# Seven half products for Q in the last block of a gated cross-attention kernel

## The reference, cut to what matters

```
Q = layernorm(x) @ Wq.T ;  K = ctx @ Wk.T ;  V = ctx @ Wv.T
P = softmax(causal(Q K^T / sqrt(128)))         4 query heads share one K and V
x = x + tanh(g_xattn) * (P V) @ Wd.T
x = x + tanh(g_ffn) * (layernorm(x) @ dequantize(qweight).T + bias)
```

## Time and profile before

| what | value |
|---|---|
| median of 3 runs | 1058.12 us |
| the profiled execution, time | 1056.85 us |
| its span, first to last instruction | 1054.9 us |
| mean granted TensorE clock | 0.995 |
| PE busy | 1017.7 us, 96% |
| DVE busy | 682.1 us, 65% |
| ACT busy | 456.6 us, 43% |
| POOL busy | 233.9 us, 22% |
| moved by DMA | 142.61 MB, mean 135 GB/s |

### The profile page before, as it was taken

The page is one execution under the profiler, slowest core; times in us unless marked ns, Lnnn a source line. Parts: engine busy times, 40 slices in busy tenths (PEclk is TensorE's granted clock), DMA queues, the critical chain, the costliest instruction groups (busy, mean ns, idle before and its releaser), DMA issues.

```text
span 1054.9 us, 19976 instructions
## 1 busy us (share of the span) xinstructions
PE 1017.7 (96%) x7842; PEld 569.2 (54%) x7842; DVE 682.1 (65%) x1374; ACT 456.6 (43%) x917; POOL 233.9 (22%) x245
## 2 busy tenths in 40 slices
PE   5889999999999999999999999999999999999995
PEld 3455555555555555555555554555555555555542
DVE  6856677777577666765466556755556664555678
ACT  5767676676533243333334333244433322333322
POOL 1355565465604000210002100210000300000013
PEclk9999999999999999999999999999999999999998
DMA  7757645445355632345422743333432443224111
GB/s 278 235 153 272 216 163 182 161 135 157 102 178 196 149 90 66 141 133 137 132 71 70 206 134 121 109 119 93 131 122 108 133 137 126 62 86 143 64 36 60
DMA packets 90219, 142.61 MB, mean 135 GB/s; under 512 B 31248, under 2 KB 64016, under 8 KB 79504
## 3 DMA queue, kind: packets, MB, share of 16 engines
q1 hardware_dynamic: 90128, 141.34, 42.0%
HBM read 94.11 MB, written 25.17 MB: 113 GB/s over the span
## 4 chain that ended last, share of the span: by engine, by line
PE 87%; DVE 7%; ACT 3%; issue 2%; DMA 1%; SPq 0%; DVEq 0%; ACTq 0%
PE pa L1295 42%; PE py L1295 30%; PE av L1408 5%; PE pp L1391 3%; PE ps L1375 2%; PE py L1466 2%; PE pp L1375 2%; DVE q L897 1%; DVE sc L943 1%; DMA raw_q<-in_wqT 1%; DVE sc L954 1%; DVE row_max L941 1%; DVE sc L937 1%; ACT q L677 1%; PE av L1442 0%
## 5 line engine op out<-in xcount | busy, mean ns | idle before, releaser
L1295 PE MATMUL pa<-xT,wq 128*128 128x512 f16 x1536 | 342.7, 379 | 9.5 <-DVE q L897 6.7
L1295 PE MATMUL py<-wd,att 128*128 128x512 f16 x1488 | 336.2, 379 | 0.8 <-issue 0.8
L1295 PEld LDWEIGHTS pa<-xT,wq 128*128 128x128 f16 x1536 | 145.8, 98 | 189.9 <-issue 22.5
L1295 PEld LDWEIGHTS py<-wd,att 128*128 128x128 f16 x1488 | 143.3, 98 | 159.1 <-issue 1.1
L677 ACT ACTIVATE q<-pa 128x512 f16<-128x512 f32 x128 | 75.7, 591 | 264.3 <-PE pa L1295 264.3
L976 DVE SCALAR_TENSOR_TENSOR xacc<-py,f_y,xacc 128x512 f32<-128x512 f32 x128 | 95.7, 747 | 125.0 <-PE py L1295 124.9
L728 ACT ACTIVATE att<-av 128x256 f16<-128x256 f32 x256 | 80.8, 384 | 145.7 <-PE av L1408 145.2
L967 DVE SCALAR_TENSOR_TENSOR att<-av,att 128x256 f16<-128x256 f32 x256 | 93.3, 416 | 67.1 <-ACT att L728 66.9
L897 DVE SCALAR_TENSOR_TENSOR q<-pa,q 128x512 f16<-128x512 f32 x128 | 87.7, 685 | 57.0 <-ACT q L677 54.2
L1295 PE MATMUL pa<-wv,cT 128*128 128x128 f16 x1536 | 96.2, 219 | 0.0
L1295 PEld LDWEIGHTS pa<-wv,cT 128*128 128x128 f16 x1536 | 89.9, 98 | 0.9
(11 more groups left out here) (131 smaller groups left out, 1060.1 us busy)
## 6 DMA issues: line engine op xcount, KB each, us to landing
wq<-kept_q SPq DMA_DIRECT2D x24, 1024.0 KB, 7.1
wd<-kept_d SPq DMA_DIRECT2D x23, 1024.0 KB, 4.8
v_dup<-v_nat SPq DMA_DIRECT2D x128, 128.0 KB, 2.4
raw_d<-in_wdT SPq DMA_DIRECT2D x8, 1024.0 KB, 10.1
kept_q<-wq SPq DMA_DIRECT2D x8, 1024.0 KB, 8.8
kept_d<-wd SPq DMA_DIRECT2D x8, 1024.0 KB, 5.4
raw_q<-in_wqT SPq DMA_DIRECT2D x7, 1024.0 KB, 5.6
wk<-kept_k SPq DMA_DIRECT2D x24, 256.0 KB, 7.3
```

The source lines that it names most:

```text
L1295: last = pe.matmul(out, stationary(a, i), moving(b, i), start=(i == 0 and (a, b) == PASSES[0]), stop=(i == count - 1 and (a, b) == PASSES[ ...
```

## The change: what it does

The names below are those of the diff. `FIRST_FAST` is 24, so `fast(m)` holds for the Q of block 3 (m = 24 to 31), which is made in steps n = 23 to 30.

- **Seven products.** For m of block 3 and each pair r of heads, the product (2 heads) x (512 features) x (512 tokens) is cut in halves along all three: head, features 0-255 or 256-511, tokens 0-255 or 256-511. Instead of eight half products it makes seven (Strassen's scheme in Winograd's form). A half product (`run`) is 2 feature chunks x 3 passes = 6 matmuls of 256 columns. Their operands are partly sums of quarters of Wq (`ws`) and of the normalised x (`tT`). Products 1, 6, 7, 4 accumulate one after another in one bank; ACT copies products 1, 5 and the sum 1+6 to SBUF in between, and the DVE adds the others to them. Each quarter then gets its high part on ACT and its low part on DVE.
- **Sums of weights.** In steps 7, 12, 13, 14, 15, 17, 18, 21 (one group each) SP loads the raw Wq of a group (`load_mix`, 1 MB), POOL makes four sums (`mix_weights`), ACT and DVE make high and low parts (`mix_hi`, `mix_lo`, four each), SP stores 1 MB (`keep_mix`). From step 22 `back_mix` loads 1 MB for each m of block 3. The squares of Wq are taken with scale 2, and `Q_SCALE` is twice what it was.
- **Sums of x.** In step 20 POOL adds quarters of the normalised block 3 (`mix_norm`, `mixed_lo`), ACT makes the high parts (`mixed_hi`); 32 more DMA transposes go out in steps 21 and 22, and 8 of the 32 of norm (1, 3) are left out.
- **Order.** Norm (1, b) of blocks 2 and 3 moves from step g = 4 to g = 3, the step of the feed-forward; its transposes go out from g = 4 on (six in g = 3 for block 3). Norm (2, 2) is made for tiles 0 and 1 in step 24 and for 2 and 3 in step 25. From step 22 on, the output parts 2 and 3 of step n are made in step n+1, between the half products (`deferred`), and `back_d(n)` goes out in the middle of step n. `ffn_zero` of block 2 moves from step 25 to step 26, ahead of `av_part`.
- **Memory.** `xs` and the mixed tiles lie in `raw_k` and `raw_v` joined; `ws`, `tT` and `raw_s` lie in `raw_q` and `raw_d`; the feed-forward's part goes to `xs` and no longer to `xn`.

```diff
+        def fast(m):
+            return FIRST_FAST <= m < STEPS
+        def deferred(n):
+            return fast(n + 2)
+        BANK_X, BANK_Y, BANK_Z = (pa[0], av[1]), (pa[1], pa[1]), (av[0], av[0])
+        MIX_STEPS = (7, 12, 13, 14, 15, 17, 18, 21)
...
+            def run(m, r, i):
...
+                elif (r, i) == (1, 5):
+                    pe.wait_ge(c12_ok, pair_count(m, 0))
+                elif (r, i) == (1, 2):
+                    pe.wait_ge(c11_ok, pair_count(m, 0))
+                elif i == 6:
+                    pe.wait_ge(p1_ok, pair_count(m, r))
+                elif i == 7:
+                    pe.wait_ge(u2_ok, pair_count(m, r))
+                elif i == 3:
+                    pe.wait_ge(p5_ok, pair_count(m, r))
+                elif i == 4:
+                    pe.wait_ge(c22_ok, pair_count(m, r))
...
+                for kc in range(2):
+                    for c, d in PASSES:
...
+                        last = pe.matmul(half(bank), a[:, c, head, w_half + kc, :], b[:, d, b_half + kc, at],
...
# TensorE, step n with fast(m)
                 score_unit(n, 0)
                 score_unit(n, 1)
+                if fast(m):
+                    run(m, 0, 1); run(m, 0, 5); run(m, 0, 2); run(m, 0, 6)
+                    y_unit(n - 1, 2)
+                    run(m, 0, 7); run(m, 0, 3); run(m, 1, 1); run(m, 0, 4)
+                    run(m, 1, 5); run(m, 1, 2); run(m, 1, 6)
+                    y_unit(n - 1, 3)
+                    run(m, 1, 7); run(m, 1, 3)
+                    p_transpose(n, 0)
+                    run(m, 1, 4)
+                    k_unit(m)
+                    p_transpose(n, 1)
+                    v_unit(m, range(TILES // 2))
+                    av_unit(n, 0); av_unit(n, 1)
+                    v_unit(m, range(TILES // 2, TILES))
+                    y_unit(n, 0); av_unit(n, 2); y_unit(n, 1); av_unit(n, 3)
...
# VectorE, the same step
+                    scores(n, 0); scores(n, 1)
+                    add_11(m, 0)
+                    normalise(n, 0)
+                    add_22(m, 0); add_12(m, 0)
+                    lo_11(m, 0); lo_22(m, 0); lo_12(m, 0)
+                    normalise(n, 1)
+                    lo_21(m, 0)
+                    p_part(n, 0)
+                    y_late(2)
+                    p_part(n, 1)
+                    add_11(m, 1)
+                    y_late(3)
+                    add_22(m, 1); add_12(m, 1)
+                    lo_11(m, 1); lo_22(m, 1); lo_12(m, 1); lo_21(m, 1)
+                    k_part(m)
+                    if g == 2 and tb == BLOCKS - 1:
+                        for t in LATE: ffn_zero(t)
...
# ScalarE, the same step
+                    copy_p1(m, 0); exp(n, 0); copy_p5(m, 0); copy_u2(m, 0); exp(n, 1)
+                    hi_11(m, 0); p_part(n, 0); hi_22(m, 0); hi_12(m, 0)
+                    copy_p1(m, 1); hi_21(m, 0); p_part(n, 1); copy_p5(m, 1); copy_u2(m, 1)
+                    hi_11(m, 1); hi_22(m, 1); hi_12(m, 1)
+                    p_transposed(n, 0)
+                    hi_21(m, 1)
+                    k_part(m)
```

More of the change, by code:

```diff
@@ L242, in norm_of, with split_norm @@
             return None
+        def split_norm(n):
+            return n % GROUPS == 0 and fast(n + 1) and n < LAST
         def wait_x_lo(eng, t):
@@ L271, in transposed @@
             else:
-                eng.wait_ge(xT_ld, 16 * 2 * KC * TILES * (call - 1))
-        def dma_tiles(n):
-            g, tb = n % GROUPS, n // GROUPS
[L278 to L282, removed]
+                eng.wait_ge(xT_ld, 16 * sum(len(transposes(c)) for c in range(2, call + 1)))
@@ new lines, in build, with quadrant, by_batch, mixing @@
+        BANK_X, BANK_Y, BANK_Z = (pa[0], av[1]), (pa[1], pa[1]), (av[0], av[0])
+        def quadrant(c, r, head, tokens):
+            return q[:, c, tokens * BPB // 2:(tokens + 1) * BPB // 2, :, 2 * r + head, :]
+        def by_batch(part):
+            return part.rearrange("p (b u s) -> p b u s", b=BPB // 2, u=HALVES)
+        MIX_STEPS = (7, 12, 13, 14, 15, 17, 18, 21)
+        MIX_ORDER = tuple((FIRST_FAST + i) % GROUPS for i in range(GROUPS))
+        def mixing(n):
+            return MIX_STEPS.index(n) if n in MIX_STEPS else None
@@ new lines, in mix_of, with transposes @@
+        def mix_of(n):
+            g, tb = n % GROUPS, n // GROUPS
+            return tb + 1 if g == 4 and FIRST_BLOCK <= tb + 1 < BLOCKS else None
+        def transposes(call):
+            return [(t, c, i) for t in range(TILES) for c in (HI, LO) for i in range(KC)
+                    if NORMS[call][0] == 2 or not fast(GROUPS * NORMS[call][1]) or t < 2 or i >= 2]
+        EARLY, FEW = 6, 5
+        MIXED = ([(t, c, i) for t in (2, 3) for c in (HI, LO) for i in range(KC)]
+                 + [(t, c, i) for i_half in ((0, 1), (2, 3)) for t in (0, 1) for c in (HI, LO) for i in i_half])
@@ new lines, in transpose_early, with load_mix @@
+            def transpose_early(n):
+                g, tb = n % GROUPS, n // GROUPS
+                if g == 3 and 0 < tb < BLOCKS - 1 and fast(GROUPS * (tb + 1)):
+                    call = NORMS.index((1, tb + 1))
+                    transpose_norm(call, transposes(call)[:EARLY])
+            def load_mix(g):
+                if g == 0:
+                    sp.wait_ge(wd_lo, HPG * (GROUPS - 1))
+                    sp.wait_ge(wd_hi, HPG * (GROUPS - 1))
+                else:
+                    sp.wait_ge(s_lo, HPG * g)
+                sp.dma_start(raw_s, wqT[MIX_ORDER[g]].rearrange("p (h n) -> p h n", h=HPG)).then_inc(s_ld, 16)
@@ L443, in _ @@
                     back_d_last()
-                if GROUPS <= n < LAST:
+                if GROUPS <= n < LAST and not fast(m):
                     back_d(n)
@@ L570, in _ @@
                     ln_rstd(call)
+                if ffn_of(n) is not None and fast(n + 1):
+                    for t in range(ffn_of(n) * TILES, (ffn_of(n) + 1) * TILES):
+                        ffn_add(t)
                 if tb == 0:
@@ new lines, in quad_hi, with hi_11, hi_22, hi_12 @@
+            def quad_hi(ready, count, r, head, tokens, part):
+                act.wait_ge(ready, count)
+                return act.activation(quadrant(HI, r, head, tokens), by_batch(part), ACT.Copy, scale=Q_SCALE)
+            def hi_11(m, r):
+                quad_hi(c11_ok, pair_count(m, r), r, 0, 0, p1[:, r, :]).then_inc(quad_hi_ok, 1)
+            def hi_22(m, r):
+                quad_hi(c22_ok, pair_count(m, r), r, 1, 1, p5).then_inc(quad_hi_ok, 1)
+            def hi_12(m, r):
+                quad_hi(c12_ok, pair_count(m, r), r, 0, 1, u2).then_inc(quad_hi_ok, 1)
@@ L821, in _ @@
                     ctx_squares(tb + 1, squares_done(g + 2) + 2 if tb == 0 else squares_done(GROUPS))
+                if mix_of(n) is not None:
+                    for t in range(TILES):
+                        mixed_hi(mix_of(n), t)
                 if call is not None:
@@ L1110, in ffn_scaled @@
                 dve.wait_ge(f_mm, t + 1)
-                bank, part = (pa, xs) if t in LATE else (py, xn)
+                if t % TILES == 0 and t > 0 and t not in FFN_DVE:
+                    dve.wait_ge(out_pool, t)
+                    if t // TILES + 2 > FIRST_BLOCK:
+                        mixed_done(dve, t // TILES + 2 - FIRST_BLOCK)
+                bank, part = pa if t in LATE else py, xn if t in FFN_DVE else xs
                 dve.tensor_tensor(part[:, t % TILES, :], bank[t % 2][:, :], ff_rows[:, SCALE_ROW, :],
```

530 lines of the change are left out of this document (437 added, 93 removed).

## The result

| | median us | lowest to highest | runs |
|---|---|---|---|
| before | 1057.54 | 1056.66 to 1060.25 | 4 |
| after | 1047.59 | 1046.94 to 1048.74 | 4 |

The ratio is 0.9906 [0.9894, 0.9918]: 9.95 us less. Forecast were 1047.9 and 10.2. The profiled execution took 1048.74 us, its span 1046.9.

The account below looks back on a forecast made before the run. TensorE, busy 96%, was taken as the bound. Gain 11.5 less stalls 1.3, others 0, is 10.2 us off 1056.85: 1046.65, with 1.27 for the median 1047.9; range 1045.0 to 1051.5, to 1055 with the broken margin.

Parts of the forecast that it names:

- Term 1: Q in 8 fast steps of block 3: fewer columns, 10.58 to 9.14 us, 1.44 a step, 11.5 us gained.
- the rival with 0.140: Q's short matmuls paced by something other than columns, 0.140 us each: 1068.8 us, slower; chance 0.05.
- the loss of 15 us: Estimate from the skill's issue gaps, some 98 ns at 256 columns: Q 6.3 to 8.2 us, kernel 15 us slower.
- The walk: Plain fast step followed engine by engine: half additions at 0.4 us, no stall, tightest place (1,4) with 0.5 us.
- a thin margin that breaks: Rival, every fast step: DVE halves cost 0.12 more each, 0.45 us a step, 3.6 in all: 1051.5; chance 0.15.
- halves at the full price: Rival: DVE halves at 0.68 each, (1,4) waits 1.5 us in all 8 steps: 1059.9, no change; chance 0.05.
- Term 2: Steps 24 and 26, extra DVE work: stalls of 0.5 and 0.8 us, together 1.3, bounds 0 and 3.
- Term 3: Sums of weights in the weight steps: taken at 0, hidden, with wd loaded in time; 8 us were cover gone.
- Term 4: Changed order, chiefly steps 11 and 19 and the transposes on SP: taken at 0, bounds 0 to 1 in each step.
- the verdict that it changes nothing outside step 26: POOL and DVE excluding each other: DVE held 1.3 us once or twice a step, sum unchanged except in step 26.
- The place that I had watched: Step 19, P V part 3 ready at 674.3, fourth output part wants it at 674.55: 0.25 us to spare.
- Sum: Whole kernel: 11.5 - 1.3 = 10.2 us off, 1046.65 for the profiled execution, 1047.9 as median; forecast's chance 0.70.

Follow-up runs that it names:

- third experiment: Kernel before with only the order exchanged in plain steps from 8 on: low part of Q's head 1 ahead of both normalises, second exponential earlier; 1052.42 us, ratio 0.9943.
- first: Kernel after with product 5 of each pair made twice, so Q has as many columns as before; 1058.52 us, ratio 1.0007 against the kernel before.
- fourth experiment: Kernel after with two more 1 MB DRAM-to-DRAM copies ahead of each raw weight load; 1065.65 us, ratio 1.0068 against the kernel before.
- ninth: Kernel after without the six early transposes of step 19, all 24 issued in step 20; 1054.39 us, ratio 0.997 against the kernel before.

## Why the prediction was right, by its steps

**Term 1, right.** Predicted 1.44 per step, measured 1.40; the period 28.8 against 28.87. The columns are 0.109 us per 256 as read from P V (12 matmuls in 1.31), and no row shows anything else pacing short matmuls: the rival with 0.140 is out. So is the loss of 15 us that the prediction had estimated from the Trainium skill (TensorE: Matmul & The Clock Gate, "Back-to-back issue gap"). The wait that goes with `q_unit` is worth 0.2 (third experiment), the columns the rest (first).

**The walk, right, and thinly so.** The DVE's half additions take 0.41 to 0.43 (0.4 taken, of 0.36 to 0.68). In step 26 `add_22` of pair 1 is done at 866.80 and product (1,4) begins at 867.27: 0.47 us to spare where 0.5 was said. So "a thin margin that breaks" and "halves at the full price" are both out, the first by half a microsecond.

**Term 2, right in place and sum.** 0.32 in step 24 (0.5) and 0.97 in step 26 (0.8), 1.29 against 1.3.

**Term 3, right for time.** Steps 13 to 18 are unchanged to 0.01 us. The sums of the weights lie in ACT's and POOL's idle time. As for `wd`: it has landed in time everywhere, in 6.1 us (median) from its issue, 4.8 before, and the fourth experiment shows that two more MB would have made it late. But of the transposes of the sums of x, which share SP's queue with it, the prediction gave no margin, and it is 2.4 us. `back_d` of step 20 went out at t = 687.34 - 678.99 = 8.35 and not 7, and some of SP's loads took 1.05 us to issue, where most took 0.38. The conclusion held, over a margin that the prediction had not looked at.

**Term 4, wrong in size.** Taken at 0, measured 0.61 + 0.32 = 0.93 us. The place that I had watched, the fourth output part of step 19, holds: with the norm's four instructions between the two parts, steps 11 and 19 are unchanged. What I had not followed is POOL. The norm, moved into this step, puts four low parts ahead of POOL's residual adds, and they run on into the next step's scores. The rule of the Trainium skill (SBUF — State Buffer, "Who interferes with whom") about POOL and DVE was in the prediction, with the verdict that it changes nothing outside step 26; the overlap that costs something lies in the scores of steps 12 and 20, which the prediction didn't walk through.

**Sum.** 11.2 - 1.29 - 0.93 = 9.0, +0.4 from the last stretch: 9.4 for the two profiled executions with an equal start. Of medians it is 9.95; the half microsecond between the two is within the spread of the start. Predicted were 10.2, 1.2 more than the steps give: 0.9 of it is the missed term 4, 0.3 the gain of 1.44 that measured 1.40. So that the medians come within 0.3 us of the forecast is in part luck; what was right is the mechanism and each term's place but the fourth's.

## What to carry to other kernels

Cost short matmuls by the shortest ones in a row in the trace, and then ask what covers the additions that replace the columns: here two output parts between the products were worth 1.8 us a step, more than the 1.4 that the seven products gained. When work is moved on an engine off the path, follow it over the end of the step on that engine too, and look for the others' instructions that read SBUF beside it. Give the queue that issues DMAs a walk of its own, with a duration per issue; its margin of 2.4 us was used up in two of the experiments.

## What the runs showed of the hardware

- Some waits of TensorE cost more than their length: 3.77 us, then 12 matmuls in 4.45 instead of 2.75 (fourth experiment); 3.61 us, then half products in 1.49 instead of 0.82 (ninth), with a granted clock of 0.50 in a part of both stretches. Waits of 1.67, 2.9 and 3.2 us made their steps longer by 1.9, 2.9 and 3.2 us.
- A DVE subtraction of 512 elements with both inputs in SBUF took 0.69 us alone, and 1.00, 1.03 and 1.30 beside POOL's adds, each time ending 0.55 us after POOL's last; its reductions, with one such input, kept 0.69 in the same stretch.
- A DMA transpose of this kind holds its queue 1.3 us. The last ones landed 2.3 us after their issue; others, issued just behind several MB of loads, took up to 10.8 us (kernel after, steps 21 and 22).
- The start of the kernel, with the same code, took 37.45 to 40.67 us over twelve profiled executions, more than most of the effects here; single executions had to be compared by steps.
